# A decoder layer on one core: value splits in two operations, layernorm epsilon and mean on GpSimd, gate bias on TensorE, two of eight expert products on ScalarE, causal masks by halves of the keys, and a new order of steps

## What is computed

```python
x = x + attn(layernorm(x))              # causal, q, k, v and output with biases
x = x + xattn(layernorm(x), ctx, mask)  # cross attention to 77 positions
x = x + ffn(layernorm(x))

def ffn(x):                             # 8 experts, the top 2 are used
    scores = maximum(x @ gate_W + gate_b, 1e-4)
    p = softmax(scores)
    _, topk_idx = top_k(p, 2)
    topk_mask = one_hot(topk_idx, 8).sum(-2) > 0
    w = maximum(p, 0.1)
    total = take_along_axis(w, topk_idx, -1).sum(-1, keepdims=True)
    comb = where(topk_mask, w / total, 0)
    y = einsum('bsd,edf->bsef', x, expert_W) + expert_b
    return einsum('bsef,bse->bsf', y, comb) / 2
```

## Time and profile before

| | us |
|---|---|
| median of 3 runs | 278.64 (277.86 to 278.95) |
| the profiled execution, its own time | 278.23 |
| its span, first instruction to last | 276.1 |
| PE busy in the span | 254.3 (92%) |
| DVE busy | 227.0 (82%) |
| ACT busy | 169.7 (61%) |
| POOL busy | 162.8 (59%) |

### The profile page before, as it was taken

The page is one execution under the profiler, slowest core; times in us unless marked ns, Lnnn a source line. Parts: engine busy times, 40 slices in busy tenths (PEclk is TensorE's granted clock), DMA queues, the critical chain, the costliest instruction groups (busy, mean ns, idle before and its releaser), DMA issues.

```text
span 276.1 us, 6407 instructions
## 1 busy us (share of the span) xinstructions
PE 254.3 (92%) x2433; PEld 123.9 (45%) x2438; DVE 227.0 (82%) x499; ACT 169.7 (61%) x224; POOL 162.8 (59%) x265
## 2 busy tenths in 40 slices
PE   7899779999999999999999999999998998997881
PEld 3388334434543354454345544345634553353340
DVE  7289998997999999999789998667987796554795
ACT  5390298597888678989979667984556225610000
POOL 6669676753649733865413481375994766069544
PEclk9999999999999999999999999999999997999979
DMA  3754134200430400711300000300003021000101
GB/s 87 211 153 130 46 98 136 73 2 6 134 99 2 114 6 5 192 40 35 84 5 5 1 2 23 99 4 2 4 1 84 14 61 40 0 2 0 38 2 38
DMA packets 19949, 14.34 MB, mean 52 GB/s; under 512 B 2720, under 2 KB 19920, under 8 KB 19920
## 3 DMA queue, kind: packets, MB, share of 16 engines
q1 hardware_dynamic: 19920, 13.94, 18.4%
HBM read 2.58 MB, written 1.05 MB: 13 GB/s over the span
## 4 chain that ended last, share of the span: by engine, by line
PE 57%; DVE 32%; POOL 4%; ACT 3%; issue 3%; POOLq 0%; DVEq 0%
PE banks L1089 11%; DVE peaks L755 9%; PE banks L1071 6%; PE banks L1111 5%; PE banks L1141 5%; PE banks L888 5%; DVE peaks L763 5%; PE banks L900 4%; PE banks L999 4%; PE banks L892 4%; PE banks L1004 4%; PE banks L1101 2%; DVE stats L722 2%; DVE xpeaks L770 2%; POOL yw L567 2%
## 5 line engine op out<-in xcount | busy, mean ns | idle before, releaser
L658 ACT ACTIVATE probs<-banks 128x1024 f32<-128x1024 f32 x80 | 79.9, 1025 | 16.7 <-PE banks L1071 15.4
L755 DVE TENSOR_REDUCE peaks<-banks 128x2 f32<-128x768 f32 (+3 forms) x77 | 82.7, 1121 | 6.8 <-PE banks L1004 5.7
L556 POOL TENSOR_SCALAR_AFFINE_SELECT probs<-probs 128x512 f32<-128x512 f32 (+1 forms) x80 | 43.8, 551 | 53.7 <-ACT probs L658 53.2
L567 POOL TENSOR_TENSOR yw<-yw 128x512 f32<-128x512 f32 (+2 forms) x42 | 34.9, 832 | 20.7 <-DVE yw L861 17.8
L1089 PE MATMUL banks<-probs,v_s 128*18 128x256 f32 (+3 forms) x512 | 42.9, 436 | 0.0
L665 ACT ACTIVATE xprobs<-banks 77x1024 f32<-77x1024 f32 x32 | 32.0, 1018 | 11.5 <-PE banks L1101 11.3
L1141 PE MATMUL banks<-expert_w_s,normed_t 128*128 128x512 f32 x64 | 34.0, 637 | 0.0
L1071 PE MATMUL banks<-q_stack,k_stack 64*128 64x512 bf16 (+3 forms) x256 | 30.0, 299 | 1.3 <-DVE peaks L755 0.6
L770 DVE TENSOR_REDUCE xpeaks<-banks 128x10 f32<-128x770 f32 (+1 forms) x24 | 23.5, 1007 | 6.0 <-PE banks L1032 3.1
L1004 PE MATMUL banks<-k_stack,q_stack 62*128 62x128 bf16 (+3 forms) x224 | 27.7, 296 | 0.0
L999 PE MATMUL banks<-causal_slot,pick_slot 64*128 64x128 bf16 (+2 forms) x308 | 25.4, 243 | 2.3 <-DVE peaks L755 1.9
(11 more groups left out here) (175 smaller groups left out, 418.3 us busy)
## 6 DMA issues: line engine op xcount, KB each, us to landing
q_stack<-parts_q SPq DMA_DIRECT2D x24, 128.0 KB, 2.4
k_stack<-parts_k SPq DMA_DIRECT2D x24, 128.0 KB, 2.4
xq_stack<-parts_x SPq DMA_DIRECT2D x24, 128.0 KB, 2.4
state<-in_x SPq DMA_DIRECT2D x4, 256.0 KB, 4.6
out<-state SPq DMA_DIRECT2D x4, 256.0 KB, 2.3
expert_w_s<-in_expert_w SPq DMA_DIRECT2D x1, 512.0 KB, 4.3
xk_stack<-parts_x SPq DMA_DIRECT2D x6, 77.0 KB
q_stack<-peaks_t SPq DMA_DIRECT2D x16, 8.0 KB
```

The source lines that it names most:

```text
L556: gp.affine_select(out=v, in_=v, compare_op=ALU.is_ge, fill=0.0, base=0, pattern=pattern, channel_multiplier=-1).then_inc(causal_done, 1)
L567: link(gp.tensor_tensor(y[:, 0:n], y[:, 0:n], y[:, n:2 * n], ALU.add))
L658: ac.activation(probs[:, grp % 2, 2 * u:2 * u + 2, :], both_banks(step), ACT.Exp, scale=SCALE).then_inc(taken_of(step), 1)
L755: ve.tensor_reduce(peaks[:, f, t, heads[0]:heads[0] + n].rearrange("p a s -> p s a"), both_banks(step)[:, :, 0:n * width].rearrange("p s ( ...
```

## The change

The constant BY_ACT = 1, 4 names the expert steps whose products move. The parts are:

- **Splits in two operations.** The subtraction writes the second bf16 part itself; `peak_rest` and `xpeak_rest` and the casts of L790 are gone (16 of them).
- **Layernorm.** DVE stops after `bn_aggr`. POOL adds epsilon itself, and normalizes as (x - mean) * rstd from `moments`, so `lowered` and `shift` are gone (12 of each on DVE and on POOL), and 12 small additions on POOL are new.
- **Gate bias on TensorE.** One fp32 matmul of 32 columns puts the bias in the bank ahead of the four gate matmuls; L820 is gone, and the maximum reads the bank.
- **`floored` and `kept` in one operation** (4 fewer on DVE).
- **Experts 1 and 4 of each batch on ACT**: four activations of 128 columns each, scaled by a column of comb, in place of one DVE product of 512 columns.
- **Masks by key halves.** A mask matmul now covers 64 keys instead of 128: c counts halves of the keys, and the weights hold, for each half, which row of the causal block a query takes. The setup has one more reduction and one small product on DVE (ahead of the first `bn_stats`), three casts instead of one, and two ACT copies, one with a bias, instead of one.
- **A new ORDER** of 525 characters, with as many warm matmuls in all (46).

```diff
-ORDER = ("2n3n46n1nnnnnnnnppppppppppppppppppppppppp...
+ORDER = ("34nn6n3nnnnnnnnpppppppppppppppp2ppppnppppxp61ppp...
...
                 if kind == "ln_stats":
-                    pool.wait_ge(var_ready, STATS[step])
+                    pool.wait_ge(moments_ready, STATS[step])
+                    link(gp.tensor_scalar(var[:, n], moments[:, n, :, 1], LN_EPS, None, ALU.add))
                     link(gp.tensor_tensor(rstd[:, n], var[:, n], minus_half[:], ALU.pow))
-                    link(gp.tensor_tensor(shift[:, n], lowered[:, n], rstd[:, n], ALU.mult))
...
-                        last = gp.tensor_scalar(normed[:, i % 2, t], state[:, b, t], rstd[:, n, t:t + 1], shift[:, n, t:t + 1],
-                                                ALU.mult, ALU.add)
+                        last = gp.tensor_scalar(normed[:, i % 2, t], state[:, b, t], moments[:, n, t, 0:1], rstd[:, n, t:t + 1],
+                                                ALU.subtract, ALU.mult)
...
-            ac.copy(causal_slot[:], banks[:, CAUSAL_BANKS[1], 0:256].rearrange("p (c k) -> p c k", c=2)).then_inc(causal_ready, 1)
+            ac.copy(causal_slot[:, 0], banks[:, CAUSAL_BANKS[1], 0:SLOT])
+            act.wait_ge(last_row_ready, 1)
+            ac.activation(causal_slot[:, 1], banks[:, CAUSAL_BANKS[1], 128 + SLOT:256], ACT.Identity, bias=last_row[:, 0:1]
+                          ).then_inc(causal_ready, 1)
...
+                elif kind == "expert" and k in BY_ACT:
+                    t, half = divmod(k, 2)
+                    n = T * b + t
+                    act.wait_ge(comb_ready, b + 1)
+                    if n >= 2:
+                        act.wait_ge(y_summed, summed_by_pool(n - 1))
+                    wait_full(act, step)
+                    for e in range(4 * half, 4 * half + 4):
+                        last = ac.activation(yw[:, t % 2, e], bank_of(step)[:, D * (e % 4):D * (e % 4) + D], ACT.Copy,
+                                             scale=g["comb"][:, t, e:e + 1])
+                    last.then_inc(taken_of(step), 1)
...
             wait_cleared(dve, "ident")
+            link(ve.tensor_reduce(slots[:], ident[:].rearrange("p (s r) -> p r s", s=2), X_AXIS, ALU.add))
+            ve.tensor_scalar(last_row[:], slots[:, SLOT - 1:SLOT], FUTURE, None, ALU.mult).then_inc(last_row_ready, 1)
...
-                    link(last)
-                    ve.tensor_scalar(var[:, n], moments[:, n, :, 1], LN_EPS, None, ALU.add)
-                    ve.tensor_scalar(lowered[:, n], moments[:, n, :, 0], -1.0, None, ALU.mult).then_inc(var_ready, 1)
+                    last.then_inc(moments_ready, 1)
...
                     link(ve.tensor_copy(part[0], src))
-                    link(ve.tensor_tensor(left, src, part[0], ALU.subtract))
-                    ve.tensor_copy(part[1], left).then_inc(done, 1)
+                    ve.tensor_tensor(part[1], src, part[0], ALU.subtract).then_inc(done, 1)
...
-                    link(ve.tensor_scalar(g["floored"][:], g["p"][:], LEAST_WEIGHT, None, ALU.max))
-                    link(ve.tensor_tensor(g["kept"][:], g["floored"][:], g["chosen"][:], ALU.mult))
+                    link(ve.scalar_tensor_tensor(out=g["kept"][:], in0=g["p"][:], scalar=LEAST_WEIGHT, in1=g["chosen"][:],
+                                                 op0=ALU.max, op1=ALU.mult))
...
+                    if bias is not None:
+                        te.matmul(bank_of(step)[:, 0:T * cols].rearrange("p (t d) -> p t d", t=T),
+                                  ident[:, 0:1].broadcast_to([128, 128]), bias[:].unsqueeze(1).broadcast_to([128, T, cols]),
+                                  start=True, stop=False, skip_group_check=True)
...
-                            diagonal = bank_of(step, s)[:, 0:n * width].rearrange("p (h k) -> p h k", h=n)[:, :, width - 128:width]
-                            te.matmul(diagonal, in_slot(pick_slot, s)[:, 128 * c:128 * c + 128],
-                                      in_slot(causal_slot, s)[:, c].unsqueeze(1).broadcast_to([SLOT, n, 128]),
+                            half = bank_of(step, s)[:, 0:n * width].rearrange("p (h k) -> p h k", h=n)
+                            half = half[:, :, width - 128 + SLOT * c:width - 128 + SLOT * c + SLOT]
+                            te.matmul(half, in_slot(pick_slot, s, SLOT)[:, 128 * c:128 * c + 128],
+                                      in_slot(causal_slot, s, SLOT)[:, c].unsqueeze(1).broadcast_to([SLOT, n, SLOT]),
                                       start=(c == 0), stop=False, skip_group_check=True)
```

48 lines of the change are left out of this document (24 added, 24 removed).

## The result

The changed kernel takes 289.44 us (median of 6 runs, 286.3 to 291.45), the kernel before 278.78 beside it: a ratio of 1.030, 95% interval 1.026 to 1.034. It is 3% slower. The prediction said 271.0, range 266.0 to 276.5, and is wrong in sign.

What follows compares the result with a forecast made beforehand. PE (57% of the chain of waits) and DVE (32%) were taken to share the bound. The terms 0 - 5.0 + 1.1 - 3.1 - 0.2 = -7.2 took 278.2 to 271.0 us, range 266.0 to 276.5.

Steps and rivals of the forecast that it cites:

- The start: Up to 31 us: DVE's gain ends in PE's wait for POOL, whose work stays the same; 0, bounds -1.0 to +0.3.
- Masks and DVE's relief: Self attention, 31 to 165 us: PE and DVE, both nearly full, each shed about 5 to 6 us; -5.0.
- the rival of narrow masks: 31 to 165 us: least matmul spacing leaves gains only in steps of four and two heads; 273.0 us, chance 10%.
- The middle: 165 to 230 us, with gates: PE gains bias matmuls and loses time to ACT's wait for comb; +1.1 us.
- Batch 2's gate to the last layernorm: 230 to 250.4 us: expert, value and score steps move inside the wait for comb; -3.1, bounds -4 and -1.
- one rival: Three batches: ACT stands at expert 1's products until comb, PE with it, clock halving behind pauses; 285 us, chance 6%.
- The end: 250.4 to 276.2 us: the gate's chain loses two short operations and gains the bias; -0.2, bounds -1.5 and +1.0.
- the fourth: Middle: the new order puts waits between full engines, leaving half of the -5.0; 275.5 us, chance 9%.
- the first three: Whole kernel: forecast 271.0 us (60%), both full engines running freer 267.2 (15%), narrow masks saving little 273.0 (10%).

Runs made afterwards that it cites:

- forms: Changed kernel with a different form of the normalization for each of the four tiles, three with a subtraction, one with an addition; 301.05 us (a single run).
- form_only: Kernel before, with lowered holding plus the mean and the normalization as multiply and subtract instead of multiply and add; 297.99 us, ratio 1.052.
- ln_add: Changed kernel with minus the mean made on POOL and the normalization as add and multiply instead of subtract and multiply; 275.21 us, ratio 0.982.
- order_only: Kernel before in the new order of steps, nothing else changed; 280.36 us, ratio 1.005.
- setup_later: ln_undone with the masks' reduction and small product on DVE behind the first statistics instead of ahead of them; 271.54 us, ratio 0.973.
- ln_undone: Changed kernel with the layernorm of before, everything else and the new order kept; 273.27 us, ratio 0.977.
- masks_back: ln_undone with the masks of before, 128 columns for a mask matmul and head; 275.52 us, ratio 0.987.
- products_back: ln_undone with the products of experts 1 and 4 of each batch back on DVE; 276.65 us, ratio 0.990.

## Why the prediction was wrong

**The failed step** is the sentence on POOL in the part on the start, "POOL does as much as before (an addition in, `shift` out)", and that the normalization has no term in the sum at all. The prediction counted POOL's instructions and took the changed one, (x - mean) * rstd, at the old one's price. `forms`, `form_only` and `ln_add` show the price: some 800 ns instead of 457, whose cause is the subtraction. With 48 of them that is a term of up to +16.5 us, which the sum put at nothing. It was an operation that the trace of before did not show, and it should have had bounds. A row gave a warning: POOL's power takes 1.03 us on 4 columns, while `shift`, a multiplication of the same shape, took 0.20, so POOL's time does depend on the operation. Another row would have misled: POOL's subtractions of two tensors (L518) take 1.16 us for 512 columns, about what a multiplication of two tensors takes (L537, 1.23 us for 616), so the price was seen in this form of instruction and not in subtraction on POOL at large.

**Why all of it reached the end.** POOL was busy 59% of the span, but nothing covers it here: the twelve layernorms stand in the chain of their batches, PE's order has the transposes at a fixed place, and PE doesn't pass them. Starts of the same step in five traces, in us:

| | before | order_only | setup_later | ln_undone | changed |
|---|---|---|---|---|---|
| power of batch 0's first layernorm | 5.8 | 5.8 | 5.8 | 6.6 | 6.6 |
| fourth power | 81.4 | 81.3 | 79.1 | 79.9 | 86.0 |
| eighth power | 161.7 | 163.1 | 158.5 | 160.1 | 169.8 |
| first, last mask step | 31.6, 161.4 | 32.5, 165.0 | 32.3, 160.8 | 33.1, 162.3 | 37.3, 171.7 |
| `g_exp` of batch 2 | 231.8 | 232.6 | 226.6 | 228.2 | 241.8 |
| last power | 250.4 | 250.7 | 243.7 | 248.5 | 258.9 |
| span | 276.1 | 277.8 | 269.3 | 272.7 | 285.6 |

Against `ln_undone` the changed kernel is 6.1 us late at the fourth power, 9.7 at the eighth, 13.6 at batch 2's gate, 10.4 at the last power and 12.9 at the end. It was caught up in part because `ln_undone` ran at half clock behind batch 2's gate (below). Against `setup_later`, whose clock held, it is 15.2 late at that gate, 15.2 at the last power and 16.3 at the end, 0.8 to 1.6 of which is the masks' setup: close to 12 x 1.37 = 16.5, less what other waits took up.

**The start, 0 (bounds -1.0 to +0.3).** It was +0.8: the first power starts at 6.6 us instead of 5.8. The two operations ahead of the first `bn_stats` were priced at 0.19 each, and the removed L727 and L728 taken off the same path. In `ln_undone`, which keeps those two, the power is at 6.6 as well. In the changed kernel the reduction and the product start at 3.51 and 3.77, the next reduction at 3.85, and the cast into `pick` behind it lasts 0.54 instead of 0.23; it reads and writes what it did. Outside the bounds, and `setup_later` gets it back.

**Masks and DVE's relief, -5.0 (bounds -6.2 to -2.5).** Too large by about 1 us. Up to the `g_exp` of batch 0, right behind this stage, `setup_later` is 3.9 us ahead of before (162.4 against 166.3) and `ln_undone` 2.4, with the start's 0.8 in it; the prediction's sum there is -5.0. In the new order, from the first mask step to the last, `order_only` takes 132.5 us, `setup_later` 128.5 and `masks_back` 131.5 (32.4 to 163.9): -4.0, of which the masks are 3.0. `setup_later` keeps L727 and L728 on DVE, and `ln_add`, which has both gone from there, takes 130.1 where `ln_undone` takes 129.2. So the mechanism held for the masks, and the layernorm's half of DVE's relief shows no gain, at least with two small operations on POOL in its place. For the whole kernel the masks are worth 0.987 - 0.973, or 4.0 us, and 2.9 with their setup's place as changed. The narrow ones start at the pace of their columns, 0.06 us for four; the rival of narrow masks falls. The Trainium skill ("TensorE: Matmul & The Clock Gate", section "Wait — 56ns, not 53.3ns?") gives some 25 ns as the least from start to start. Counted for every matmul, as the prediction applied it, the trace doesn't agree: four of them, two pairs side by side in the halves of the rows, take 0.06 us, 15 ns each. Counted for each half of the rows, with 30 ns from one matmul to the next, the trace agrees.

The split's saving was near what was counted, though two rows side by side don't show it:

```profile
L806 DVE TENSOR_TENSOR xpeak_parts<-xpeaks,xpeak_parts 128x32 bf16<-128x32 f32 x8 | 3.6, 454 | 0.3
L806 DVE TENSOR_TENSOR peak_parts<-peaks,peak_parts 128x32 bf16<-128x32 f32 x8 | 3.0, 371 | 0.3
```

Before, subtraction and cast took 300 + 266 ns (peaks: L789, L790) and 266 + 297 (cross attention). But these times move with what runs beside them: the unchanged fp32 subtraction of `xpeaks` takes 266 ns before and 417 in `order_only`. In one order, the new one, the whole split goes from 0.997 to 0.766 us for the peaks and from 1.056 to 0.766 for cross attention (`order_only` against `ln_undone`), 0.23 and 0.29 saved where 0.27 and 0.30 were counted. What a bf16 output costs by itself can't be read from these rows.

**The middle, +1.1.** The sign was wrong here. From the `g_exp` of batch 0 to that of batch 2 it takes 65.5 us before, 66.0 in `order_only` and 64.2 in `ln_undone` and `setup_later`: -1.3. Up to there the prediction's sum is 0 - 5.0 + 1.1 = -3.9; `ln_undone` has -3.6 and `setup_later` -5.2, so the sum looks better than its terms. `products_back` takes 64.8, so moving the products gives 0.6 here, where the prediction had put PE's loss by them at +1.0. ACT's wait for comb was 0.68 us in batch 1 and none in batch 2, and not 2 to 3; the long one, 5.13 us, is in the last batch, where ACT has nothing else to do. The bias took 1.5 us of PE's time in four gates of `ln_undone`, 0.37 each (0.25 predicted), and ACT's four activations 1.14 (1.3 predicted). Over the changed kernel ACT rose by 7.7 us, to 177.4, and DVE fell by 13.9, to 213.1, not to some 210.

**Batch 2's gate to the last layernorm, -3.1.** From `g_exp` to the last power: 18.6 us before, 17.1 in `setup_later`, where the clock stays at 1.00: -1.5. The clock of before is 0.95 in this stretch, so up to 0.9 of the 1.5 may be the clock and not the order; the changed kernel, too, takes 17.2 at 1.00. In `ln_undone` it is 20.4, +1.8, with the clock at 0.50 in the windows from 227 to 236 us. The prediction carried the row with 0.92 over to a stage in which PE waits at other places, and had no term for the clock but in one rival. Whether the spread between executions of one kernel lies here isn't shown, since each kernel has one trace.

**The end, -0.2.** From the last power to the end of the span: 25.7 us before, 25.6 in `setup_later`, 24.2 in `ln_undone`, 26.7 in the changed kernel, whose last normalization is 1.4 longer. That `ln_undone` is shorter here by 1.4 than `setup_later` isn't explained.

Without the layernorm's part the change gives 273.3 us, 2.3 above the forecast and inside the range, and with the masks' setup moved 271.5. The sum was nearly right for the kernel without the part that had no price, and in part by luck: in `setup_later` the span falls by 6.8 us where the sum has 7.2, as -3.9, -1.3, -1.5 and -0.1 where the prediction had -5.0, +1.1, -3.1 and -0.2. The chances, too, don't fit the cases: "most of the fourth" adds more than the 0.02 that 0.87 leaves beside the first three. The range, which was drawn around terms that were looked at, could not hold that part.

## What to carry to other kernels

When an instruction stays but its arithmetic changes, it is a new instruction: give it bounds of its own, and on GpSimd prefer add and multiply with a negated operand to a subtraction, at least until one trace has shown both. Multiply what a change costs in one layernorm by the number of times that a chain passes through it, whatever the busy share of the engine says. Parts that shed or move work may be worth nothing in the old order and over 2% in a new one that by itself gives nothing (1.000 and 1.005 of before apart, 0.977 together), so they have to be measured in the order that they will have.
